# The last two groups of a quantized feed-forward layer: finer pieces, accumulating DMAs for three residuals, and halves stored from two queues

## The reference

```python
x, itok = (64, 64, 512) f32, (64,) int32; weights (200, 64, 64); weight (512, 512); bias (512,)
w = weights[itok]                        # one 64x64 matrix per batch row
y = einsum('bct,bcd->bdt', x, w)         # the mix, f32
a = quant_dequant_mxfp4(y)               # blocks of 32 along the last dimension
b = quant_dequant_mxfp4(weight)
out = x + einsum('mk,nk->mn', a, b) + bias
```

## Time and profile before

| | us |
|---|---|
| median of 3 runs | 98.33 |
| lowest, highest | 97.95, 99.38 |
| the profiled execution | 97.9 |
| its span, first to last instruction | 96.2 |
| TensorE, VectorE, ScalarE, GpSimd busy | 84.4, 81.9, 75.3, 32.9 |
| DMA moved, mean | 22.17 MB, 230 GB/s |

### The profile page before, as it was taken

How to read it: one execution, slowest core, us unless ns; L and a number is a source line. 1 busy time by engine, 2 the same in 40 slices (tenths; PEclk the granted TensorE clock), 3 DMA queues, 4 the chain that set the end, 5 groups by cost and what they waited for, 6 DMA issues and landing times.

```text
span 96.2 us, 2263 instructions
## 1 busy us (share of the span) xinstructions
PE 84.4 (88%) x715; PEld 41.2 (43%) x715; DVE 81.9 (85%) x138; ACT 75.3 (78%) x85; POOL 32.9 (34%) x60
## 2 busy tenths in 40 slices
PE   5999594999799998999899899989999989989800
PEld 4966252595482324344233433333352333445300
DVE  1248999999999999999999999999979999885600
ACT  4740498699998869999999999999999849957000
POOL 4273758399647548303000300320040021054000
PEclk9999999999999999999999999999999999999995
DMA  1898789694896789799999991896579399486992
GB/s 34 288 316 295 244 249 301 212 352 125 181 317 218 274 248 269 242 312 265 254 310 298 311 212 49 272 245 116 218 185 224 114 263 222 88 272 175 270 285 92
DMA packets 13901, 22.17 MB, mean 230 GB/s; under 512 B 4034, under 2 KB 4802, under 8 KB 13890
## 3 DMA queue, kind: packets, MB, share of 16 engines
q1 hardware_dynamic: 11456, 17.31, 56.4%
q0 software_dynamic: 2432, 4.73, 23.6%
q10 hardware_dynamic: 2, 0.00, 0.0%
HBM read 10.49 MB, written 8.39 MB: 196 GB/s over the span
## 4 chain that ended last, share of the span: by engine, by line
PE 44%; ACT 11%; DVE 10%; issue 6%; ACTq 0%; DVEq 0%
PE o_ps L357 20%; PE y_ps L357 5%; PE y_ps L306 5%; ACT y_sb L471 5%; ACT o_sb L493 4%; PE o_ps L352 4%; PE o_ps L337 3%; DVE a L654 3%; DVE n_int L625 2%; DVE top L645 2%; ACT z L463 1%; PE o_ps L382 1%; PE y_ps L367 1%; PE y_ps L300 1%; PE y_ps L318 1%
## 5 line engine op out<-in xcount | busy, mean ns | idle before, releaser
L357 PE MATMUL o_ps<-wT,aT 128*128 128x512 bf16 x100 | 23.8, 380 | 0.4 <-ACT aT L508 0.4
L183 POOL DMA_DIRECT2D mix<-in_L_cond_weights_dram x32 | 17.9, 560 | 12.4 <-issue 11.0
L625 DVE TENSOR_TENSOR n_int<-y_sb,inv 128x1024 int16<-128x1024 f32 (+1 forms) x17 | 19.5, 1155 | 0.2
L306 PE MATMUL y_ps<-x_sb,mix 64*64 64x512 f32 x120 | 15.6, 606 | 3.9 <-DMA mix<-in_L_cond_weights_dram 2.4
L272 POOL DMA_DIRECT2D x_sb<-o_sb x6 | 6.1, 1014 | 35.1 <-ACT o_sb L493 35.1
L382 PE MATMUL o_ps<-idle 128*128 128x128 bf16 x214 | 16.6, 235 | 1.2 <-DVE idle L664 1.2
L463 ACT ACTIVATE z<-y_ps 128x1024 bf16<-128x1024 bf16 x16 | 16.2, 1039 | 1.5 <-PE y_ps L306 1.2
L471 ACT COPY y_sb<-y_ps 128x1024 f32<-128x1024 f32 x16 | 16.3, 1035 | 0.0
L382 PEld LDWEIGHTS o_ps<-idle 128*128 128x128 bf16 x214 | 13.6, 105 | 5.1 <-issue 4.7
L480 ACT ACTIVATE zone<-inv 128x1024 int16<-128x1024 int16 (+2 forms) x11 | 11.6, 1074 | 3.8 <-DVE inv L618 3.8
L502 ACT COPY aT<-o_ps 128x1024 bf16<-128x1024 bf16 x14 | 13.7, 1045 | 1.0 <-PE o_ps L337 1.0
(11 more groups left out here) (52 smaller groups left out, 76.0 us busy)
## 6 DMA issues: line engine op xcount, KB each, us to landing
x_sb<-in_x_dram SPq DMA_DIRECT2D x7, 1024.0 KB, 6.4
out_dram<-x_sb SPq DMA_DIRECT2D x15, 256.0 KB, 3.6
x_sb<-o_sb POOLq DMA_DIRECT2D x6, 512.0 KB, 5.2
out_dram<-x_sb SPq DMA_DIRECT2D x6, 512.0 KB, 3.1
w_sb<-in_L_ffn_weight_dram SPq DMA_DIRECT2D x4, 256.0 KB, 3.4
x_sb<-in_x_dram SPq DMA_DIRECT2D x2, 512.0 KB, 6.6
out_dram<-x_sb POOLq DMA_DIRECT2D x4, 256.0 KB, 3.6
mix<-in_L_cond_weights_dram POOLq DMA_DIRECT2D x32, 16.0 KB, 4.5
```

The lines of the kernel that those rows point to most:

```text
L183: queue.dma_start(mix[HALVES[i % 2], first + i // 2, :], table[bass.ds(row, 1), :, :].rearrange("o c d -> (o c) d")).then_inc(mix_in[step] ...
L306: last = nc.tensor.matmul(y_ps[HALVES[g], 2 * q + r, :], mix[HALVES[r], (step - 1) * GROUP + n, :], x_tiles(step, n)[HALVES[r], :], start= ...
L357: last = nc.tensor.matmul(o_bank(step, t), aT[:, t, c, :], wT[:, c, :], start=False, stop=(c == KC - 1))
L625: nc.vector.tensor_tensor(columns(n_int, t, n), columns(y_sb[:, step % 2, :, :], t, n), columns(inv, t, n), ALU.mult).then_inc(n_done, 1)
```

## The change

It touches the two ends. At the start ScalarE issues the first loads of x between its operations on W's first tiles, `load_mixes` leaves out the check of row numbers, SyncE issues group 2's matrices ahead of its x, and W's first half goes through inverse, codes and turn before its second half. At the end all of group 8 is mixed in exchanged form and its x loaded a second time in that form (`last_x`). Group 7's codes come in two halves and are turned in `y_ps`; its residuals on TensorE go: tiles 0 and 1 (from a new buffer `late_sb`) and tile 2 get theirs by accumulating DMAs, tile 3 from VectorE. GpSimd's queue then stores tiles 2 and 3 of group 6 (before SyncE's) and tiles 0 to 2 of group 7. Group 8's codes, turns and copies go tile by tile, and each finished tile is stored in two halves of 64 partitions, the lower by SyncE, the upper by ScalarE.

The core of the diff; `after(step)` and `late_part(part)` are counts of semaphores, `top_zone`, `invert`, `limit` and `rescale` get a first tile and a number of tiles, and `zone_pair` is `zone_group` with explicit counts:

```diff
+        late_sb = sb("late_sb", [P, 2, N], F32)
+        last_x = sb("last_x", [P, GROUP, T], F32)
...
+                return o_ps[:, 2 + q, :].bitcast(BF16)
+            return y_ps[:, 3 - q, :].bitcast(BF16)
...
-            return o_ps[:, 0, :] if t == 0 else y_ps[:, t - 1, :]
+            return (o_ps[:, 0, :], o_ps[:, 3, :], y_ps[:, 0, :])[t]
...
-                cond_sb[:, 2 * first:2 * (first + len(tiles))], engines=[engine], min_val=0, max_val=S - 1)
+                cond_sb[:, 2 * first:2 * (first + len(tiles))], engines=[engine], min_val=0, max_val=S - 1,
+                skip_runtime_bounds_check_because="cond holds row numbers of the table")
...
+        def store_last(queue, t, g, part, done):
+            queue.dma_start(exchanged_dram[LAST - 1, t // 2, g, t % 2, :, part], last_x[HALVES[g], t, part]
+                            ).then_inc(done, 16)
...
-            for h in range(2):
-                sp.dma_start(x_tiles(1, 2 * h, 2).rearrange("p (n t) -> p n t", n=2),
-                             x_dram[:, 2 * h:2 * h + 2, :]).then_inc(x_first_in[h], 16)
             sp.wait_ge(cond_in, 16)
             load_mixes(sp, mybir.EngineType.SP, sp_mix_in, 1, SP_TILES)
+            load_mixes(sp, mybir.EngineType.SP, sp_mix_in, 2, SP_TILES)
             load_x(2)
-            load_mixes(sp, mybir.EngineType.SP, sp_mix_in, 2, SP_TILES)
             load_x(3)
...
+            for q in range(2):
+                for g in range(2):
+                    sp.dma_start(last_x[HALVES[g], 2 * q:2 * q + 2, :],
+                                 exchanged_x_dram[LAST - 1, q, g, :, :, :].rearrange("r c t -> c r t")
+                                 ).then_inc(last_x_in, 16)
...
+                if step < LAST - 2:
+                    sp.wait_ge(x_added[step % 2], 16 * ((step + 1) // 2))
+                    store(step, SUMMED, GROUP - SUMMED)
+            sp.wait_ge(added, 1)
+            store(LAST - 1, GROUP - 1)
             for t in range(GROUP - 1):
-                sp.wait_ge(added, t + 1)
-                store(LAST, t)
+                sp.wait_ge(added, t + 2)
+                store_last(sp, t, 0, slice(0, N), stored)
             for half in range(2):
-                sp.wait_ge(added, GROUP + half)
-                sp.dma_start(out_dram[:, TILES - 1, n_half(half)], x_tiles(LAST, GROUP - 1)[:, n_half(half)]
-                             ).then_inc(stored, 16)
-            sp.wait_ge(stored, 16 * (3 * (LAST - 2) + GROUP + 1))
-            sp.wait_ge(late_stored, 16 * 2 * 2)
+                sp.wait_ge(added, GROUP + 1 + half)
+                store_last(sp, GROUP - 1, 0, n_half(half), stored)
...
-            for q in range(2):
-                pool.wait_ge(late_copied, 2 * q + 2)
-                for g in range(2):
-                    pool.dma_start(exchanged_dram[LAST - 2, q, g, :, :, :].rearrange("r c t -> c r t"),
-                                   x_tiles(LAST - 1, 2 * q, 2)[HALVES[g], :].rearrange("p (r t) -> p r t", r=2)
-                                   ).then_inc(late_stored, 16)
+            pool.wait_ge(late_copied, 2)
+            pool.dma_start(x_tiles(LAST - 1, 0, 2), late_sb[:, :, :].rearrange("p t n -> p (t n)"), accum_op=ALU.add
+                           ).then_inc(late_added, 16)
+            pool.wait_ge(late_tile, 1)
+            pool.dma_start(x_tiles(LAST - 1, SUMMED), o_sb[:, (LAST - 1) % 2, 0, :], accum_op=ALU.add
+                           ).then_inc(x_added[(LAST - 1) % 2], 16)
+            pool.wait_ge(x_added[(LAST - 2) % 2], 16 * ((LAST - 1) // 2))
+            n0 = (LAST - 3) * GROUP + SUMMED
+            pool.dma_start(out_dram[:, n0:n0 + 2, :], x_tiles(LAST - 2, SUMMED, 2).rearrange("p (n t) -> p n t", n=2)
+                           ).then_inc(late_stored, 16)
+            pool.wait_ge(late_added, 16)
+            n0 = (LAST - 2) * GROUP
+            pool.dma_start(out_dram[:, n0:n0 + 2, :], x_tiles(LAST - 1, 0, 2).rearrange("p (n t) -> p n t", n=2)
+                           ).then_inc(late_stored, 16)
+            pool.wait_ge(x_added[(LAST - 1) % 2], 16 * (LAST // 2))
+            pool.dma_start(out_dram[:, n0 + SUMMED, :], x_tiles(LAST - 1, SUMMED)).then_inc(late_stored, 16)
...
-                if step == LAST and q == 1:
-                    for n in (2 * q, 2 * q + 1):
-                        for half in HALVES:
-                            last = nc.tensor.matmul(y_ps[half, n, :], mix[half, (step - 1) * GROUP + n, :],
-                                                    x_tiles(step, n)[half, :], start=True, stop=True)
-                        last.then_inc(y_ready, 1)
-                    return
...
-            keep_busy(24)
+            pe.wait_ge(a2_done, 1)
+            turn_pair(0, 0, straight=True)
+            keep_busy(32)
             for q in range(2):
                 mix_pair(2, q)
-            pe.wait_ge(ident_ready, 1)
-            for q in range(2):
-                pe.wait_ge(a2_done, q + 1)
-                turn_pair(0, q, straight=True)
-            keep_busy(60)
+            pe.wait_ge(a2_done, 2)
+            turn_pair(0, 1, straight=True)
+            keep_busy(56)
...
-            residual_pair(LAST - 1, 1)
-            for t in range(GROUP):
-                bias_tile(LAST - 1, t, start=False)
+            pe.wait_ge(a2_done, late_part(0))
+            turn_pair(LAST - 1, 0)
+            for t in range(2):
+                bias_tile(LAST - 1, t)
+            pe.wait_ge(a2_done, late_part(1))
+            turn_pair(LAST - 1, 1)
+            for t in range(2):
+                ffn_tile(LAST - 1, t)
+            pe.wait_ge(aT_ready, tiles_done(LAST - 1, 3))
+            for t in range(2, GROUP):
+                bias_tile(LAST - 1, t)
+            for t in range(2, GROUP):
+                ffn_tile(LAST - 1, t)
+            pe.wait_ge(pair_copied, 2 * (LAST - 2))
             bias_tile(LAST, 0)
-            for t in range(GROUP):
-                ffn_tile(LAST - 1, t)
-            pe.wait_ge(a2_done, LAST + 2)
-            turn_pair(LAST, 0)
+            turn_last(0)
+            pe.wait_ge(copied_out, 2 * (LAST - 2))
+            turn_last(1)
+            bias_tile(LAST, 1)
...
+            bias_half(0)
+            pe.wait_ge(late_tile, 1)
+            bias_half(1)
             ffn_tile(LAST, 2)
-            pe.wait_ge(late_copied, 4)
             for half in range(2):
...
+            def copy_late():
+                act.wait_ge(o_ready, tiles_done(LAST - 1, 1))
+                nc.scalar.copy(late_sb[:, :, :], y_ps[:, 0:2, :]).then_inc(late_copied, 2)
...
+            def copy_late_tile():
+                act.wait_ge(x_added[(LAST - 1) % 2], 16 * ((LAST - 2) // 2))
+                act.wait_ge(o_ready, tiles_done(LAST - 1, SUMMED))
+                nc.scalar.copy(o_sb[:, (LAST - 1) % 2, 0, :], o_bank(LAST - 1, SUMMED)).then_inc(late_tile, 1)
...
+                act.dma_start(x_tiles(1, 2 * t, 2).rearrange("p (n t) -> p n t", n=2),
+                              x_dram[:, 2 * t:2 * t + 2, :]).then_inc(x_first_in[t], 16)
+            for t in range(2, GROUP):
+                z_w(t)
+            zone_pair(1, 0)
+            z_pair(1, 0)
+            zone_pair(2, 0, 2)
+            z_pair(1, 1)
             for q in range(2):
                 y_pair(1, q)
+            for t in range(2):
+                copy_w(t)
...
+            zone_pair(after(LAST - 1), after(LAST - 2))
+            y_pair(LAST, 1)
+            copy_pair(LAST - 2)
+            copy_turned(LAST - 1, 0)
+            copy_out(LAST - 2)
+            copy_turned(LAST - 1, 1)
+            for t in range(GROUP - 1):
+                zone_pair(after(LAST), late_part(1), t, 1)
+            copy_late()
+            copy_late_tile()
             copy_turned_last(0)
-            copy_turned_last(1)
-            copy_late(1)
-            copy_turned_last(2)
-            copy_turned_last(3)
+            zone_pair(after(LAST), late_part(1), GROUP - 1, 1)
+            for t in range(1, GROUP):
+                copy_turned_last(t)
+            for t in range(GROUP - 1):
+                act.wait_ge(added, t + 2)
+                store_last(act, t, 1, slice(0, N), others_stored)
+            for half in range(2):
+                act.wait_ge(added, GROUP + 1 + half)
+                store_last(act, GROUP - 1, 1, n_half(half), others_stored)
...
+            for t in range(2):
+                tree_1(0, t, 1, z_count=t + 1)
+                tree_2(t + 1, t, 1)
             tree_3(2, 0, 2)
             block_max(1, 0, 2)
+            lowest_zone(1, 0, 2)
+            lift(0, 1, 0, 2)
+            top_zone(1, 0, 2)
+            invert(1, 0, 2)
...
+            round_y(LAST - 1, 0)
+            round_y(LAST - 1, 2)
+            tree_1(LAST)
+            other_zones(LAST - 1)
+            tree_2(LAST + 3)
+            limit(LAST - 1, after(LAST - 1), 0, 2)
+            tree_3(LAST + 3)
+            rescale(LAST - 1, late_part(0), 2 * LAST, 0, 2)
+            block_max(LAST + 2)
```

(14 more changed lines are left out.)

222 lines of the change are left out of this document (96 added, 126 removed).

## The result

| | us | ratio to before |
|---|---|---|
| forecast | 99.1 (96.0 to 101.0) | |
| changed kernel, median | 102.81 (101.75 to 105.66) | 1.039 [1.033, 1.045] |
| the same, second measurement | 101.74 (101.02 to 102.65) | 1.030 [1.018, 1.041] |
| the same, third measurement | 102.52 (101.26 to 103.58) | 1.035 [1.025, 1.046] |
| before, beside each | 98.14, 98.53, 98.88 | |

The change is slower by 3 to 4%, outside the range. Ratios leave out executions that a lower granted clock disturbed; the medians hold them, and the profiled one of the first measurement (103.58 us) is one. I read the end from the profiled execution of the second measurement: 102.08 us, span 100.2, against 97.9 and 96.2 before. The start is read from all three profiles.

What follows compares the result with a forecast made beforehand. The prediction took storing by the DMA engines to bound the end: 3.40 MB from 84.1 in 11.6 us, 1.7 to the last landing, span 97.4, plus 1.7 around it, gave 99.1 us (96.0 to 101.0).

Steps and rivals of the forecast that it cites:

- Direction of the mechanism: At the end, 2.6 us of earlier compute are lost in the DMA queue; span 97.4 against 96.2, 1.2 us more.
- The start: Up to group 1's codes: first mix near 10.8 instead of 11.60, 0.2 us gained, from 0.7 lost to 0.4 gained.
- the prediction's own signs: At the start, wrong if the first mix is not before 11.3 or group 1's turn not between 25.6 and 26.7.
- the price of storing: At the end, from 84.1: 3.40 MB at 293 GB/s takes 11.6 us, so moving ends at 95.7.
- The price of the split: At the start, W's second zones stand between ScalarE's `z` operations, so `tree_1(1)` begins 4.2 us after the first mix.
- the rival that the start loses: At the start, tables land no earlier because x moves beside them: 0.6 us later, 99.9 us in all; chance 0.11.
- The compute path: At the end, group 8's last addition comes 2.4 us earlier, 2.6 with the start.
- the 1.7 us put behind it: At the end, 1.7 us from the end of moving to the span's end, as before: 95.7 + 1.7 = 97.4.
- The 11.1 us that I had summed by kinds: Tail transfers at each kind's best rate: accumulation 4.1 us, full stores 4.0, half stores 3.0.
- the single rate of 293 GB/s: Rate taken for all 3.40 MB in the tail: the old tail's 275 GB/s at 0.94 busy, when full.
- The half-height rival: At the end, group 8's half-height stores on two queues don't overlap: 5.1 us instead of 3.6, 100.6 in all; chance 0.22.
- The tail doesn't bind: At the end, accumulation and stores overlap better and the last store decides: 94.8 us in all; chance 0.17.

Runs made afterwards that it cites:

- a_noacc: Changed kernel with tiles 0 to 2 of group 7 stored without residuals, no accumulating DMA there: 97.69 us, ratio 0.993.
- b_start: Kernel before with only the change's transfers at the start (issue order, no row-number checks), operations in old order: 97.90 us, ratio 0.996.
- e_before_sp: Kernel before with the change's transfers at the start, and group 7's second pair stored by SyncE instead of GpSimd: 96.84 us, ratio 0.986.
- a_issue_old: Changed kernel with the start's transfers issued in the old order with row-number checks, W's codes still split: 103.02 us, ratio 1.044.
- b_acc: Kernel before with group 7's residuals taken off TensorE and added by two accumulating DMAs of 0.52 MB: 104.12 us, beside 98.50 for before.
- d_copy: Changed kernel with both accumulating DMAs of group 7 made plain copies between the same buffers: 99.09 us, ratio 1.004.
- c_te: Changed kernel without group 7's accumulating DMAs: residuals of tiles 0 and 1 on TensorE, tile 2's on VectorE: 99.48 us, ratio 1.012.
- c_te_whole: Changed kernel with group 7's residuals on TensorE and VectorE, and group 8 stored at whole height by SyncE alone: 98.42 us, ratio 0.994.

## Why the prediction was wrong

- **Direction of the mechanism: right.** The tail is bound by the DMA engines, they are full from 84.4 on, and the 2.2 us of earlier compute are lost there (a_noacc, which is free of accumulation, keeps 0.7%).
- **The start: wrong by the prediction's own signs, and a smaller loss than the price of storing below.** The first mix was to come near 10.8. In the twelve profiles with the changed start it came at 11.26 to 12.84, before 11.3 in one of them; the turn of group 1 came at 26.22 to 28.18, median 26.9, against 26.09 before. The row was read rightly, but taking the checks out did not bring the tables sooner: without them the mix came at 11.64 and 11.84 with the old order of operations (b_start, e_before_sp), with them at 11.60, 11.48 and 10.82 (before, a_issue_old, b_acc). The price of the split was right: `tree_1` of group 1 starts 15.41 - 11.26 = 4.15 us behind the mix, forecast 4.2, and 3.61 before. With the price and without the gain, the rival that the start loses came closer than the forecast. How much of the time it makes isn't shown, since no run takes the split of W back; by the medians of the turns, 26.9 against 26.1, it is an estimated 0.8 us at most.
- **The compute path: right.** Last addition forecast at 88.8, found at 89.29. Counted from the turn of group 1 it comes at 63.1 us in all three profiles, against 65.4 before: 2.3 us gained, 2.4 forecast. The loop of ScalarE's copies still takes 51.98 - 43.31 = 8.67 us a step.
- **The step that failed is the price of storing**, "3.40 / 0.293 = 11.6 us. Moving ends at 84.1 + 11.6 = 95.7", and the 1.7 us put behind it. In the profiled execution, whose span of 100.2 is 2.8 above the forecast 97.4:
  - Moving started at 84.4 instead of 84.1 (0.3), as the turn came at 26.22 instead of 25.9.
  - It took 0.912 of 13.8 us, 12.6, instead of 11.6 (1.0). The amount was right: 3.42 MB. So was the rate of accumulation, 0.18 MB/us against the 0.19 taken from the earlier trace rows. The 11.1 us that I had summed by kinds was low because the other two queues took 0.327 x 13.8 = 4.5 us for 1.30 MB, not 3.7; the single rate of 293 GB/s, which was in fact 3.42 / 12.6 = 271, did not cover it.
  - From the end of moving, 97.0, to the end were 3.2 us instead of 1.7 (1.5). The "1.7 later, by the last landing" was taken over from a kernel whose last transfer was a SyncE store that lands in 3.5 us. Now the last landing came at 98.7, 1.7 behind the end of moving instead of 1.3, and then another 1.5 instead of 0.4: there stood GpSimd's drain, which in the old kernel ended at 88.3 + 7.65 = 95.95, just by SyncE's 95.8, and so could not be seen as a term. GpSimd's last store now stands behind an accumulation, 2.6 us later, and the end moved with it.
- **What the accumulations cost in all**, by a_noacc 4.05 us, is more than the 0.78 / 0.293 = 2.7 us that they are in my sum. d_copy splits it, roughly: 2.6% of the time for adding, 1.1% for moving. My sum gave the two the same price, that of an average byte, while the row of 0.19 MB/us stood beside it. That is the lesson in the working.
- **The half-height rival** was the likeliest slower case, at 100.6. Its price of 1.5 us was measured at 0.8, 1.1 and none by the medians of three pairs (0.4%, 1.8% and none by the ratios). It isn't the cause of the loss: a_noacc keeps these halves and is no slower than before. The Trainium skill, "DMA: Bandwidth & Descriptors", "Rules for kernel authors", holds that disjoint halves aren't worth two transfers; two of the three pairs agree in sign, and the third, with engines as full, shows no price.
- **The tail doesn't bind** fell: full engines from 84.4 to 96.5.
- The forecast's own time was also made against an execution 0.4 us under the median of before; the three medians of after, 101.7 to 102.8, are 2.6 to 3.7 us above 99.1.

Three things stay open. What the start costs in the time was not measured. Why c_te is 1.2% slower than before isn't shown: c_te_whole, which keeps GpSimd's store in halves and its later store of tile 2, is as fast as a_noacc, so these cost only together with group 8's halves. And why GpSimd's drain ends 2 us after its last landing, where SyncE goes on after 0.2, isn't shown.

## What to carry to other kernels

When transfers of different kinds share a full tail, price each by its own share of the engines, not by an average rate: an accumulating DMA between buffers held them twice as long per byte as a copy. Moving work off a compute engine into DMAs paid nothing here, where the DMA engines had no room, and compute that ended earlier in front of a full queue gave little. Look at the end of every engine's block: a last DMA on GpSimd that lands among the last can hold the end back after every transfer has landed. One profile is not enough for a start that waits for small transfers; here the first mix differed by 1.6 us between profiles of one kernel.

## What the runs showed of the hardware that was not expected

- GpSimd's drain at the end of its block ended 2.0 to 2.2 us after the landing of its last DMA in all seventeen profiles, whatever its length (5.83 us in e_before_sp, 7.65 in the kernel before, 9.14 in the changed kernel). In the changed kernel's three profiles SyncE stood 1.1 to 1.3 us for it after everything had landed.
- A GpSimd addition of two SBUF buffers (128x1024 f32, 2.52 us) held a VectorE operation beside it until it was over: 2.56 us instead of 0.42.
- The issue of a store can be slow: SyncE's five halves of group 8 took 0.97 to 2.38 us each in the changed kernel and 0.49 to 1.57 in a_noacc, with engines as full, against 0.35 us for its store at 86.38. What sets it isn't shown.
